# A recurrent layer on 8 cores: the hidden activations of the feed-forward stage transposed by DMA instead of by TensorE and ScalarE

## The chip, the cores and the metric

One Trainium2 chip, all 8 of its cores. Each core runs the same program on one of 8 sequences of 4096 tokens, with no traffic between cores. The metric is the device time of the slowest core in microseconds (us).

## What is computed

The layer is a spectral mixer times a gated feed-forward. The part that the change touches is the feed-forward with block quantisation:

```python
def block_quant(v, m_bits, bk):          # blocks of bk=32 along K share an exponent
    vb = v.reshape(*lead, K // bk, bk)
    amax = max(abs(vb)); e = floor(log2(amax)); scale = exp2(e - m_bits)
    return (round(vb / scale) * scale).reshape(v.shape)

def lowprec_linear(x, w, b, m_bits, bk):
    return einsum('bsk,nk->bsn', block_quant(x), block_quant(w)) + b

xn = layernorm(x)                        # (8, 4096, 1024)
h = gelu(lowprec_linear(xn, w_fc, b_fc)) # 1024 -> 4096
g = silu(lowprec_linear(h, w_proj, b_proj))   # 4096 -> 1024
out = x + spectral_mixer(xn) * g
```

The spectral mixer (a Fourier transform of chunks of 64 tokens, an attention over the low frequencies, a causal convolution over the high ones, and the inverse transform) is computed in later stages and is not changed.

## The kernel before

The program is written by hand: `B` collects for each engine a list of instructions in the order in which they are emitted, `b.wait` adds a wait on a semaphore to one engine's list, `b.inc` and `b.seal` add an increment. Every engine runs its list in order, so an instruction behind a wait waits too. SP is the engine whose queue issues nearly all DMAs; GpSimd issues a few later loads of weights. T, V and S are the semaphores that TensorE, VectorE and ScalarE raise.

The stages are: quantising and transposing the weights (lines 380 to 415), the feed-forward stage (lines 435 to 671), the Fourier stage and the convolution, the attention, and the inverse transform with the output. A full barrier stands between the first two and after the second.

The feed-forward stage runs over 32 tiles `i` of 128 tokens. All quantised weights are in SBUF (`WfcqT`, `WpjqT`). For each tile the 4096 hidden columns are taken in four quarters `w` of 1024:

- `hmm(w)`: up-projection of a quarter, 16 matmuls of 128x512 and two for the bias, from `xqT_t` into PSUM banks of `psA` (two quarters fit).
- `gelu(w)`: two ScalarE activations from PSUM into `hb_t` (two slots).
- `v_amax`, `q_scales`, `v_apply`: VectorE finds the block maxima, makes the scales, and writes the quantised bf16 quarter into `hq_t` (two slots), tokens on partitions.
- `t_tr(w)`: TensorE transposes the quarter by eight matmuls with the identity (`t_transpose8`, line 347) into PSUM banks 0 and 1 of `psB`.
- `s_te(w)`: ScalarE copies the eight blocks into `hqT_t` (`s_evac8`, line 357), hidden columns on partitions. `hqT_t` has one slot, 128x1024.
- `t_f(w)`: down-projection of the quarter, 16 matmuls of 128x512 that accumulate in banks 2 and 3 of `psB`, with `hqT_t` as weights; behind quarter 3 two for the bias.

TensorE's order in a tile is up-projections 0, 1, 2; transposes 0, down-projection 0, up-projection 3, transposes 1, down-projection 1, transposes 2, down-projection 2, transposes 3, down-projection 3, the transposes of the next tile's quantised input (`xq_t` to `xqT_t`), and then the next tile. ScalarE copies quarter 0 before GELU 2, and quarter 1 before GELU 3. VectorE quantises a quarter only after it has made the scales of the next. At the tile's end ScalarE applies SiLU to the sum, and SP stores it (`g_t` to `g_s`, line 670). SP also stores the normalised input (`xnb_t` to `xnb_s`, line 615) and loads the tile after next (`xt`, line 598). These three are all that SP issues in a tile.

Of the kernel before, what the change touches and what calls it, by code (L numbers as in the profile page):

```python
# [118 lines left out]
def build_program(phases=4, p2sub=9):  # L119
# [35 lines left out]
    def sb(name, shape, dtype, stack):  # L155
        return stack.enter_context(nc.sbuf_tensor(name, list(shape), dtype))
# [18 lines left out]

    b = B()
    for s in ("cst", "gq", "T", "V", "S", "wst0", "wst1", "x0", "x1",
              "xnbst", "gst", "p2x0", "p2x1", "p4l0", "p4l1", "p4s0", "p4s1", "bld", "bspl"):
        b.add_sem(s, esg.enter_context(nc.semaphore("sem_" + s)))

    def bankA(k, w=512):
# [2 lines left out]
    def bankB(k, w=512):  # L184
        return psB.ap()[:, 512 * k:512 * k + w]
# [111 lines left out]
    def q_views(src_ap, nblk, dst_ap, acol, tcol):  # L297
        W = 32 * nblk
        rs = rsq.ap()[:, acol:acol + nblk]
        sc = scq.ap()[:, acol:acol + nblk]  # L300
        return {
            "a": amx.ap()[:, acol:acol + nblk],
            "y": yq.ap()[:, acol:acol + nblk],
            "e32": e32q.ap()[:, acol:acol + nblk],
            "rs": rs, "sc": sc,
            "src3": src_ap.rearrange("p (nb k) -> p nb k", k=32),
            "tw": tb.ap()[:, tcol:tcol + W],
            "iw": ib.ap()[:, tcol:tcol + W],
            "t3": tb.ap()[:, tcol:tcol + W].rearrange("p (nb k) -> p nb k", k=32),
            "i3": ib.ap()[:, tcol:tcol + W].rearrange("p (nb k) -> p nb k", k=32),  # L310
            "dst3": dst_ap.rearrange("p (nb k) -> p nb k", k=32),
            "rs3": rs.unsqueeze(2).broadcast_to([128, nblk, 32]),
            "sc3": sc.unsqueeze(2).broadcast_to([128, nblk, 32]),
        }

    def q_amax(qv):
        b.plain("vector", lambda e: e.tensor_reduce(  # L317
            qv["a"], qv["src3"], axis=AX.X, op=AluOpType.max,
            apply_absolute_value=True))
        qv["vA"] = b.seal("vector", "V")  # L320

    def q_scales(qv):
        b.plain("vector", lambda e: e.drain())
        b.plain("vector", lambda e: e.tensor_scalar_max(qv["a"], qv["a"], 1e-37))
        b.plain("vector", lambda e: e.drain())
        b.plain("vector", lambda e: e.tensor_scalar(
            qv["e32"], qv["a"].bitcast(I32), 0x7F800000, None,
            op0=AluOpType.bitwise_and))
        b.plain("vector", lambda e: e.drain())
        b.plain("vector", lambda e: e.tensor_scalar_mul(  # L330
            qv["sc"], qv["e32"].bitcast(F32), 0.125))
        b.plain("vector", lambda e: e.drain())
        b.plain("vector", lambda e: e.reciprocal(qv["rs"], qv["sc"]))
        b.plain("vector", lambda e: e.drain())
        qv["sB"] = None

    def q_apply(qv):
        b.plain("vector", lambda e: e.tensor_tensor(  # L338
            qv["t3"], qv["src3"], qv["rs3"], op=AluOpType.mult))
        b.plain("vector", lambda e: e.drain())  # L340
        b.plain("vector", lambda e: e.tensor_copy(qv["iw"], qv["tw"]))  # L341
        b.plain("vector", lambda e: e.drain())
        b.plain("vector", lambda e: e.tensor_tensor(  # L343
            qv["dst3"], qv["i3"], qv["sc3"], op=AluOpType.mult))
        qv["done"] = b.seal("vector", "V")

    def t_transpose8(src_bf_ap):
        for blk in range(8):
            bank = blk // 4
            o = psB.ap()[:, 512 * bank + 128 * (blk % 4):  # L350
                         512 * bank + 128 * (blk % 4) + 128]
            sblk = src_bf_ap[:, 128 * blk:128 * blk + 128]
            b.plain("tensor", lambda e, o=o, l=sblk:
                    e.matmul(o, l, I128b.ap(), start=True, stop=True))  # L354
        return b.seal("tensor", "T")

    def s_evac8(dst_views, tT):
        b.wait("scalar", "T", tT)
        for blk in range(8):
            bank = blk // 4  # L360
            s = psB.ap()[:, 512 * bank + 128 * (blk % 4):
                         512 * bank + 128 * (blk % 4) + 128]
            b.plain("scalar", lambda e, o=dst_views[blk], s=s: e.copy(o, s))  # L363
        return b.seal("scalar", "S")
# [63 lines left out]
    hq_t = sb("hq_t", (128, 2048), BF16, es01)  # L428
    hqT_t = sb("hqT_t", (128, 1024), BF16, es01)
# [5 lines left out]
    chk = {}  # L435
# [71 lines left out]
    for i in range(NTILES):  # L507
# [41 lines left out]
                           hq_t.ap()[:, hs:hs + 1024], 32 + 32 * (w % 2), 0)  # L549

        def t_tr(w):
            b.wait("tensor", "V", chk[(i, w, "ap")])
            chk[(i, w, "tr")] = t_transpose8(hq_t.ap()[:, (w % 2) * 1024:
                                                       (w % 2) * 1024 + 1024])

        def s_te(w):
            chk[(i, w, "te")] = s_evac8(
                [hqT_t.ap()[:, 128 * j:128 * j + 128] for j in range(8)],
                chk[(i, w, "tr")])

        def t_f(w):
            b.wait("tensor", "S", chk[(i, w, "te")])
            if w == 0 and (i - 1, "sil") in chk:
                b.wait("tensor", "S", chk[(i - 1, "sil")])
            for K in range(8):
                lhs = hqT_t.ap()[:, 128 * K:128 * K + 128]
                for c2 in range(2):
                    rhs = WpjqT.ap()[:, D * (8 * w + K) + 512 * c2:
                                     D * (8 * w + K) + 512 * c2 + 512]
                    st = (w == 0 and K == 0)  # L570
                    b.plain("tensor", lambda e, o=bankB(2 + c2), l=lhs, r=rhs,
                            st=st: e.matmul(o, l, r, start=st, stop=False))  # L572
            if w == 3:
                for c2 in range(2):
                    rhs = bspl_pj.ap()[:, 512 * c2:512 * c2 + 512]
                    b.plain("tensor", lambda e, o=bankB(2 + c2), r=rhs:
                            e.matmul(o, ones2.ap(), r, start=False, stop=True))
            chk[(i, w, "f")] = b.seal("tensor", "T")
# [4 lines left out]
            chk[(i, w, "am")] = qh["vA"]  # L583

        def v_apply(w, qh):
            if (i, w - 2, "tr") in chk:
                b.wait("vector", "T", chk[(i, w - 2, "tr")])
            elif (i - 1, w + 2, "tr") in chk:
                b.wait("vector", "T", chk[(i - 1, w + 2, "tr")])
            q_apply(qh)  # L590
            chk[(i, w, "ap")] = qh["done"]

# [25 lines left out]
        v_amax(1, qh[1])  # L618
        q_scales(qh[1])
        v_apply(0, qh[0])  # L620
        t_tr(0)
        s_te(0)
        t_f(0)
        hmm(3)
        gelu(2)
        qh[2] = mk_qh(2)
        v_amax(2, qh[2])
        q_scales(qh[2])
        v_apply(1, qh[1])
        t_tr(1)  # L630
        s_te(1)
        t_f(1)
        gelu(3)
        qh[3] = mk_qh(3)
        v_amax(3, qh[3])
        q_scales(qh[3])
        v_apply(2, qh[2])
        t_tr(2)
        s_te(2)
        t_f(2)  # L640
        v_apply(3, qh[3])
        t_tr(3)
        s_te(3)
        t_f(3)
        if nx < NTILES:
            qx = q_views(xn_t.ap()[:, ((nx % 2) * 1024):((nx % 2) * 1024) + 1024],
                         32, xq_t.ap()[:, ((nx % 2) * 1024):((nx % 2) * 1024) + 1024],
                         0, 1024)
            q_amax(qx)
            q_scales(qx)  # L650
            if (i - 1, "xqT") in chk:
                b.wait("vector", "T", chk[(i - 1, "xqT")])
            q_apply(qx)
            b.wait("tensor", "V", qx["done"])
            b.wait("tensor", "S", chk[(i, 3, "te")])
            chk[(nx, "xqT")] = t_transpose8(
                xq_t.ap()[:, ((nx % 2) * 1024):((nx % 2) * 1024) + 1024])
            chk[(nx, "xqTe")] = s_evac8(
                [xqT_t.ap()[:, ((nx % 2) * 1024) + 128 * j:
                            ((nx % 2) * 1024) + 128 * j + 128] for j in range(8)],  # L660
                chk[(nx, "xqT")])
# [421 lines left out]
    for p in range(NPAIR):  # L1083
        sl = (p % 2) * 1024
# [111 lines left out]
```

How the kernel before makes its waits and increments, by code:

```python
    def inc(self, eng, make, sem, n=1):  # L88
        h = self.sem[sem]
        self.ops[eng].append(lambda e, make=make, h=h, n=n: make(e).then_inc(h, n))
        self.c[sem] += n
        return self.c[sem]
# [4 lines left out]
    def seal(self, eng, sem, n=1):  # L97
        h = self.sem[sem]
        last = self.ops[eng].pop()
        self.ops[eng].append(lambda e, last=last, h=h, n=n:
                             last(e).then_inc(h, n))
        self.c[sem] += n
        return self.c[sem]
# [1 line left out]
    def wait(self, eng, sem, val=None):  # L105
        h = self.sem[sem]
        v = self.c[sem] if val is None else val
        if v > 0:
            self.ops[eng].append(lambda e, h=h, v=v: e.wait_ge(h, v))
        return v
```

## Time and profile before

| | |
|---|---|
| time, median of 2 runs | 3848.76 us (3847.25 to 3850.28) |
| the profiled execution's own time | 3850.36 us |
| its span on the slowest core (core 5) | 3848.8 us |
| spans of the 8 cores | 3832.5 to 3848.8 us |
| busy: TensorE matmul, VectorE, ScalarE | 1897.9 (49%), 1584.8 (41%), 945.6 us (25%) |
| feed-forward stage | 672 to 2539 us |
| largest line of the chain that ended last | down-projection, L572: 12% |

The profile is that of one execution on the slowest core. Engines are PE (TensorE matmul), PEld (its weight loads), DVE (VectorE), ACT (ScalarE), POOL (GpSimd) and SP; SPq is SP's queue issuing a DMA. L572 is line 572 of the kernel; a helper's line stands for all that call it, so L354 is every transposing matmul and L363 every copy behind one. PEclk or the granted clock is TensorE's clock as a share of full speed (2.4 GHz).

### The profile page before, as it was taken

Reading aid. Unit: us, or ns where it says so; the run is one execution under the profiler, and the core shown is the slowest. Engines: PE = TensorE matmul, PEld = TensorE weight load, DVE = VectorE, ACT = ScalarE, POOL = GpSimd, SP = SyncE. Lnnn points to the kernel's source line nnn. Section 1 sums busy time; section 2 is a strip of 40 time slices with the busy share of each in tenths; the row PEclk is TensorE's granted clock in tenths of the full one; section 3 lists DMA queues with packets and bytes.
Section 4 is the critical chain, followed back from the end, with each engine's and each line's share of the span. In section 5 each row is a group of like instructions: output and inputs, shape, how many; then the busy total and the mean of one; then the engine's idle time right before and its main releaser. Section 6 shows DMA issues by size and latency. Waiting matters only on the chain.

```text
span 3848.8 us, 33385 instructions; the slowest of 8 cores (3832.5 to 3848.8 us)
## 1 busy us (share of the span) xinstructions
PE 1897.9 (49%) x10624; PEld 978.9 (25%) x10624; DVE 1584.8 (41%) x3175; ACT 945.6 (25%) x2925; POOL 29.9 (1%) x60
## 2 busy tenths in 40 slices
PE   0111101676676676676676667632777224233333
PEld 0000000222232232222222222222666212111211
DVE  4555554545445455455454554442233011221212
ACT  0111111333333323333333333310111032321111
POOL 0000000000000000000000000000000100000000
PEclk9999999888888888888888888865888655555555
DMA  1111111000000000000000000034010500014443
GB/s 43 55 55 55 50 54 55 25 25 17 28 22 20 28 21 21 28 18 24 28 14 28 28 14 28 14 72 104 23 29 23 88 0 1 0 43 143 143 144 139
DMA packets 62580, 168.28 MB, mean 44 GB/s; under 512 B 9923, under 2 KB 10179, under 8 KB 62408
## 3 DMA queue, kind: packets, MB, share of 16 engines
q1 hardware_dynamic: 54344, 151.47, 12.4%
q0 software_dynamic: 8064, 14.68, 2.5%
q8 instruction: 88, 1.44, 0.2%
q14 instruction: 84, 0.69, 0.1%
HBM read 138.84 MB, written 41.94 MB: 47 GB/s over the span
## 4 chain that ended last, share of the span: by engine, by line
PE 36%; DVE 23%; ACT 15%; DMA 14%; issue 7%; SPq 2%; DVEq 2%; POOL 1%; ACTq 0%; POOLq 0%
PE psB L572 12%; PE psA L525 7%; ACT hqT_t L363 5%; DMA gp<-g_s 4%; DVE tb L338 4%; DVE amx L317 4%; DMA wstg<-wproj 3%; PE psB L354 3%; DMA wstg<-wfc 3%; PE psA L857 3%; PE psB L875 3%; ACT hb_t L543 3%; DVE ib L341 2%; DVE hq_t L343 2%; DVE wqb L343 2%
## 5 line engine op out<-in xcount | busy, mean ns | idle before, releaser
L572 PE MATMUL psB<-WpjqT,hqT_t 128*128 128x512 bf16 x2048 | 592.4, 455 | 220.2 <-ACT hqT_t L363 220.2
L525 PE MATMUL psA<-WfcqT,xqT_t 128*128 128x512 bf16 x2048 | 505.7, 404 | 54.1 <-ACT xqT_t L363 54.1
L317 DVE TENSOR_REDUCE amx<-hb_t 128x32 f32<-128x1024 f32 x128 | 156.2, 1220 | 789.0 <-ACT hb_t L543 789.0
L363 ACT CAST hqT_t<-psB 128x128 bf16<-128x128 f32 x1024 | 186.2, 303 | 962.4 <-PE psB L354 962.3
L572 PEld LDWEIGHTS psB<-WpjqT,hqT_t 128*128 128x128 bf16 x2048 | 222.6, 113 | 554.6 <-issue 418.1
L354 PE MATMUL psB<-I128b_sb,wqb 128*128 128x128 bf16 x512 | 64.7, 306 | 597.7 <-DVE wqb L343 597.7
L525 PEld LDWEIGHTS psA<-WfcqT,xqT_t 128*128 128x128 bf16 x2048 | 203.2, 103 | 337.0 <-issue 143.1
L354 PE MATMUL psB<-I128b_sb,hq_t 128*128 128x128 bf16 x1024 | 102.1, 259 | 294.7 <-DVE hq_t L343 294.7
L354 PEld LDWEIGHTS psB<-I128b_sb,wqb 128*128 128x128 bf16 x512 | 49.5, 137 | 612.6 <-issue 612.6
L317 DVE TENSOR_REDUCE amx<-wstg 128x32 f32<-128x1024 f32 x64 | 78.1, 1220 | 251.5 <-DMA wstg<-wproj 129.0
L1135 DVE TENSOR_TENSOR ub<-psB,gp 128x1024 f32<-128x1024 f32 x32 | 39.2, 1225 | 329.7 <-PE psB L1129 329.7
L354 PEld LDWEIGHTS psB<-I128b_sb,hq_t 128*128 128x128 bf16 x1024 | 79.4, 116 | 345.6 <-issue 338.1
L1121 PE MATMUL psB<-xnb,I128b_sb 128*128 128x512 bf16 x64 | 32.4, 609 | 266.1 <-DMA gp<-g_s 266.1
L341 DVE CAST ib<-tb 128x1024 int32<-128x1024 f32 x224 | 155.5, 694 | 17.2 <-issue 0.9
L338 DVE TENSOR_TENSOR tb<-hb_t,rsq 128x1024 f32<-128x1024 f32 x128 | 156.7, 1224 | 14.2 <-issue 1.0
L343 DVE TENSOR_TENSOR hq_t<-ib,scq 128x1024 bf16<-128x1024 int32 x128 | 156.8, 1225 | 9.9 <-issue 0.4
L543 ACT ACTIVATE hb_t<-psA 128x512 f32<-128x512 f32 x256 | 145.1, 643 | 2.4 <-PE psA L529 1.7
L1112 ACT CAST slotR<-psA 66x512 bf16<-66x512 f32 x64 | 34.1, 582 | 357.5 <-PE psA L1102 357.5
L363 ACT CAST WfcqT<-psB 128x128 bf16<-128x128 f32 x256 | 46.5, 303 | 292.2 <-PE psB L354 292.2
L363 ACT CAST WpjqT<-psB 128x128 bf16<-128x128 f32 x256 | 46.6, 303 | 262.2 <-PE psB L354 262.1
L983 DVE TENSOR_TENSOR Ssb<-psB,maskt 128x256 f32<-128x256 f32 x64 | 24.2, 420 | 206.3 <-PE psB L976 206.3
L861 ACT ACTIVATE Hbt<-psA 128x232 bf16<-128x232 f32 x128 | 46.5, 364 | 253.2 <-PE psA L857 253.2
(122 smaller groups left out, 2461.9 us busy)
## 6 DMA issues: line engine op xcount, KB each, us to landing
wstg<-wfc SPq DMA_DIRECT2D x32, 512.0 KB, 3.5
wstg<-wproj SPq DMA_DIRECT2D x32, 512.0 KB, 3.7
xt<-x SPq DMA_DIRECT2D x32, 512.0 KB, 5.3
g_s<-g_t SPq DMA_DIRECT2D x32, 512.0 KB, 3.6
xnbp<-xnb_s SPq DMA_DIRECT2D x64, 256.0 KB, 2.6
xp<-x SPq DMA_DIRECT2D x32, 512.0 KB, 4.8
gp<-g_s SPq DMA_DIRECT2D x32, 512.0 KB, 5.3
out<-ob SPq DMA_DIRECT2D x32, 512.0 KB, 3.0
```

What stands on the lines that cost most here:

```text
L317: b.plain("vector", lambda e: e.tensor_reduce(qv["a"], qv["src3"], axis=AX.X, op=AluOpType.max, apply_absolute_value=True))
L338: b.plain("vector", lambda e: e.tensor_tensor(qv["t3"], qv["src3"], qv["rs3"], op=AluOpType.mult))
L341: b.plain("vector", lambda e: e.tensor_copy(qv["iw"], qv["tw"]))
L343: b.plain("vector", lambda e: e.tensor_tensor(qv["dst3"], qv["i3"], qv["sc3"], op=AluOpType.mult))
L354: e.matmul(o, l, I128b.ap(), start=True, stop=True))
L363: b.plain("scalar", lambda e, o=dst_views[blk], s=s: e.copy(o, s))
L525: st=(K == 0): e.matmul(o, l, r, start=st, stop=False))
L543: s=bankA(pb + c2): e.activation(o, s, AF.Gelu))
L572: st=st: e.matmul(o, l, r, start=st, stop=False))
L857: sp=(j == KS - 1): e.matmul(o, l, r, start=st, stop=sp))
L861: s=bankA(pb2)[:, 0:GW]: e.activation(o, s, AF.Gelu))
L875: sp=(K == 7): e.matmul(o, l, r, start=st, stop=sp))
```

## The change

The transposes of the quantised quarters leave TensorE and ScalarE. `t_tr` now issues eight DMA transposes of 128x128 bf16 from SP's queue, from `hq_t` to `hqT_t`, both in SBUF, on one of two new semaphores. Before the eight, SP waits until VectorE has written the quarter and until TensorE has ended the down-projection before it, since `hqT_t` still has one slot. `s_te` does nothing. `t_f` waits for the DMA semaphore in place of ScalarE's. `v_apply` may overwrite a slot of `hq_t` once the down-projection of two quarters ago has ended, where it waited for its transposes before. The transposes of the input tile (`xq_t`) stay on TensorE, without their wait for the copies of quarter 3.

```diff
     for s in ("cst", "gq", "T", "V", "S", "wst0", "wst1", "x0", "x1",
-              "xnbst", "gst", "p2x0", "p2x1", "p4l0", "p4l1", "p4s0", "p4s1", "bld", "bspl"):
+              "xnbst", "gst", "p2x0", "p2x1", "p4l0", "p4l1", "p4s0", "p4s1", "bld", "bspl",
+              "htr0", "htr1"):
...
         def t_tr(w):
-            b.wait("tensor", "V", chk[(i, w, "ap")])
-            chk[(i, w, "tr")] = t_transpose8(hq_t.ap()[:, (w % 2) * 1024:
-                                                       (w % 2) * 1024 + 1024])
+            sem = "htr%d" % (w % 2)
+            sl = (w % 2) * 1024
+            b.wait("sync", "V", chk[(i, w, "ap")])
+            if (i, w - 1, "f") in chk:
+                b.wait("sync", "T", chk[(i, w - 1, "f")])
+            elif (i - 1, 3, "f") in chk and w == 0:
+                b.wait("sync", "T", chk[(i - 1, 3, "f")])
+            for k in range(8):
+                b.inc("sync", lambda e, k=k, sl=sl: e.dma_start_transpose(
+                    hqT_t.ap()[:, 128 * k:128 * k + 128],
+                    hq_t.ap()[:, sl + 128 * k:sl + 128 * k + 128]), sem, 16)
+            chk[(i, w, "te")] = (sem, b.c[sem])
 
         def s_te(w):
-            chk[(i, w, "te")] = s_evac8(
-                [hqT_t.ap()[:, 128 * j:128 * j + 128] for j in range(8)],
-                chk[(i, w, "tr")])
+            pass
 
         def t_f(w):
-            b.wait("tensor", "S", chk[(i, w, "te")])
+            sem, v = chk[(i, w, "te")]
+            b.wait("tensor", sem, v)
...
         def v_apply(w, qh):
-            if (i, w - 2, "tr") in chk:
-                b.wait("vector", "T", chk[(i, w - 2, "tr")])
-            elif (i - 1, w + 2, "tr") in chk:
-                b.wait("vector", "T", chk[(i - 1, w + 2, "tr")])
+            if (i, w - 2, "f") in chk:
+                b.wait("vector", "T", chk[(i, w - 2, "f")])
+            elif (i - 1, w + 2, "f") in chk:
+                b.wait("vector", "T", chk[(i - 1, w + 2, "f")])
...
             b.wait("tensor", "V", qx["done"])
-            b.wait("tensor", "S", chk[(i, 3, "te")])
```

## Rows read from the trace of the kernel before

**Rows 1.** Stages: stretch, its length, PE, PEld, DVE, ACT, POOL busy, PEclk, DMA, GB/s

```profile
672.00:2539.00 1867.00, 1286.77 (x5696) 537.23 (x5696) 929.24 (x1438) 618.73 (x1852) 0.00 (x0) 0.83 0.07 22
...
3230.00:3849.00 619.00, 220.05 (x1104) 123.69 (x1104) 120.34 (x205) 121.94 (x276) 0.00 (x0) 0.54 0.27 95
```

**Rows 2.** The chain that ended last, over one tile: start us, us, what

```profile
1496.50 5.22 PE psA L525 x16
...
1515.18 1.24 DVE hq_t L343
...
1519.36 5.73 PE psB L572 x16
...
1528.55 0.53 PE psA L529 x2
...
1534.85 1.22 DVE tb L338
...
1536.92 1.24 DVE hq_t L343
...
1540.99 5.16 PE psB L572 x16
...
1548.29 3.61 PE psB L572 x16
1551.90 0.53 PE psB L577 x2
...
1554.68 5.14 PE psA L525 x16
```

**Rows 3.** Timeline of the same tile: start us, us, engine, line, what

```profile
1518.92 1.18 ACT L543 ACTIVATE hb_t<-psA 128x512 f32<-128x512 f32 x2
...
1519.75 0.15 PEld L572 LDWEIGHTS psB<-WpjqT,hqT_t 128*128 128x128 bf16 x1 [0.28 <-issue]
1520.17 0.15 PEld L572 LDWEIGHTS psB<-WpjqT,hqT_t 128*128 128x128 bf16 x1 [0.28 <-issue]
...
1530.99 1.18 ACT L543 ACTIVATE hb_t<-psA 128x512 f32<-128x512 f32 x2
```

**Rows 4.** The page's groups of instructions: busy, mean ns | idle before, releaser

```profile
L572 PE MATMUL psB<-WpjqT,hqT_t 128*128 128x512 bf16 x2048 | 592.4, 455 | 220.2 <-ACT hqT_t L363 220.2
...
L354 PE MATMUL psB<-I128b_sb,hq_t 128*128 128x128 bf16 x1024 | 102.1, 259 | 294.7 <-DVE hq_t L343 294.7
```

**Rows 5.** Two stretches of the tile, columns as in rows 1

```profile
1510.44:1519.36 8.92, 1.01 (x8) 0.80 (x9) 5.26 (x8) 1.70 (x9) 0.00 (x0) 0.67 0.08 29
1519.36:1529.08 9.72, 9.72 (x36) 3.72 (x36) 5.27 (x8) 0.74 (x2) 0.00 (x0) 0.78 0.01 2
```

**Rows 6.** Line 293, copies SBUF to SBUF of 2 KB: issue ns min/median/max, landing

```profile
L293 SPq DMA_DIRECT2D bspl_fc<-bst_hi x4: 497/497/617, 16.6 to 31.9; - x4
L293 SPq DMA_DIRECT2D bspl_fc<-bst_lo x4: 562/575/575, 17.2 to 32.4; - x4
...
DMA to landing us min/median/max: 1.6/1.7/1.7
```

**Rows 7.** Timeline of SP's queue, first in the prelude, then in a tile

```profile
21.63 0.50 SPq L293 DMA_DIRECT2D bspl_fc<-bst_hi  x1
22.17 0.57 SPq L293 DMA_DIRECT2D bspl_fc<-bst_lo  x1
22.79 0.51 SPq L220 DMA_DIRECT2D bst_f<-bfc  x1
...
1499.23 0.38 SPq L220 DMA_DIRECT2D xt<-x  x1
1510.10 0.32 SPq L615 DMA_DIRECT2D xnb_s<-xnb_t  x1
```

**Rows 8.** DMA issues by line: KB each, median us from issue to landing

```profile
xnb_s<-xnb_t SPq DMA_DIRECT2D x32, 256.0 KB, 2.0
```

**Rows 9.** DMA queues in the first 17 us: packets, MB, share of 16 engines

```profile
q1 hardware_dynamic: 3328, 0.41, 16.2%
```

## Prediction

> **What bounds the kernel now.** I began with the table of stages, the busy time of each engine in a stretch [rows 1]. The change touches only the feed-forward stage, 672 to 2539 us: 1867 us, in which TensorE is busy 1287, VectorE 929, ScalarE 619 and the DMA engines 7%. No engine fills it, so the stage is a chain that hands over from engine to engine. The chain of one token tile [rows 2] runs from the first matmul of the up-projection at 1496.50 to the same matmul of the next tile at 1554.68: 58.18 us, and 32 of them are 1862 us, the whole stage. So the question is what one tile's chain becomes, times 32.
>
> The reader should cut this chain into pieces. (a) 1496.50 to 1516.42, 19.92 us: up-projection 0, two GELUs with their table loads, scales, and the quantised hq_t of quarter 0 ready (1515.18 + 1.24). (b) hq_t ready to the start of down-projection 0 at 1519.36, 2.94 us: eight transposing matmuls and eight ScalarE copies. (c) down-projection 0, 5.73 us. (d) up-projection 3 behind it, 3.98 us, to 1529.07. (e) from there to hq_t of quarter 2 ready at 1538.16: the transposes and copies of quarter 1, then GELU 3 at 1530.99 [rows 3], then VectorE for 7.17 us. (f) 2.83 us of transposes and copies to down-projection 2 at 1540.99, 5.16 us long. (g) 2.14 us to down-projection 3 at 1548.29. (h) 4.15 us with its bias, to 1552.44. (i) 2.24 us for the transposes of the next input tile. The waits [rows 4] say the same in totals: TensorE stands 220.2 us for the copies into hqT_t and 294.7 us for hq_t.
>
> **The change, part by part.** A tile's 4096 hidden columns are done in four quarters. Removed: per quarter, eight 128x128 matmuls on TensorE and eight copies on ScalarE. In the chain they stand as 2.94 us (quarter 0), about 1.9 us ahead of GELU 3 (quarter 1: 1529.07 to 1530.99), 2.83 and 2.14 us. Their busy time is otherwise no gain, since neither engine is full [rows 1].
>
> Added: per quarter, eight DMA transposes from SP's queue, SBUF to SBUF, 32 KB each, 1024 in all. Call T the time from the moment they may start (hq_t ready and the earlier down-projection ended) to the moment the next down-projection may start, with all eight landed. It replaces (b), (f) and (g) directly.
>
> Moved: hqT_t is one buffer. Before, TensorE could put quarter w in PSUM and ScalarE copied it within 2 us. Now SP waits until down-projection w-1 has ended and only then starts eight transfers, so that from quarter 1 on T lies wholly between two down-projections. Only for quarter 1 is there cover: up-projection 3, 3.98 us of T. For quarters 2 and 3 hq_t is ready early if T is long, so T stands bare. TensorE works in order, so while it waits at down-projection 0, up-projection 3 waits too, and with it GELU 3.
>
> New chain of a tile. Down-projection 0 starts at 19.92 + T. Its end is 5.73 later. Down-projection 1 starts T after that end. Quarter 2's hq_t is ready 3.98 + 0.1 + 7.17 = 11.3 us after it (no copies ahead of GELU 3). With down-projection 1 at 5.7 us, the transposes of quarter 2 start at the later of 11.3 and T + 5.7: from T = 5.6 on, the down-projection sets it. Then T, 5.7, T, 5.7 + 0.55 of bias, and 2.24.
> For T over 5.6: 19.92 + 5.73 + 5.7 + 5.7 + 6.25 + 2.24 + 4T = 45.5 + 4T.
> For T under 5.6: 19.92 + 5.73 + 11.3 + 5.7 + 6.25 + 2.24 + 3T = 51.1 + 3T, which equals 58.2 at T = 2.3.
>
> The 5.7 is a choice. After the idle stretches before down-projections 0 and 2 the sixteen matmuls took 5.73 and 5.16 us, where they take 3.61 after 2.14 us of hand-over [rows 2]. The table of one tile shows why [rows 5]: in the stretch with the long idle time the granted clock fell to 0.67, and the projection after it started low (1.2 GHz) and rose to 2.4 on the way: one weight load to the next is 0.43 us there [rows 3]. With an idle stretch of T before each of them I give every down-projection the 5.7 us of the first. If the clock stays low throughout, sixteen take 16 x 0.43 = 6.9, about 1.1 us more for each of four. That is possible: the last stage, 36% busy in short bursts, was granted 0.54 [rows 1].
>
> **What is T?** No row shows a DMA transpose, so it needs two bounds. The nearest rows are copies SBUF to SBUF from the same queue, 2 KB each: 0.50 to 0.58 us of the queue for one, a pitch of about 0.6 us in a row, 1.6 to 1.7 us from issue to landing [rows 6, 7]. If eight transposes pipeline like that, T = 7 x 0.6 + 1.7 + 0.1 = 6.0. If one ends before the next begins, T = 8 x 1.7 = 13.6. Lower still would be the plain loads' and stores' 0.32 to 0.38 us of queue [rows 7]: 7 x 0.36 + 1.7 = 4.2. Higher would be a serial row of transfers that land as the 256 KB store does, 2.0 us [rows 8]: 16. Moving the bytes is not the limit by any row: in the first 17 us 3328 small packets took 16.2% of 16 engines, 13 ns each [rows 9].
> A transpose has to be cut up by the queue into more pieces than a copy of one row, so its issue should be longer than 0.6 us, but full serialisation would be the worst a queue does. I take the middle of 6.0 and 13.6, T = 9.8, which is 1.2 us for each transpose.
> That a transpose costs a queue more than its bytes is not shown by any row. The Trainium skill, VectorE: DVE Perf Modes, "The three transpose paths", gives 1309 ns for a 128x128 bf16 transpose by DMA against 390 ns on TensorE, and so speaks against this change. As an estimate from that page, 8 x 1.31 = 10.5 us for T, the total would be near 4790 us.
>
> Other queue effects. SP holds three plain transfers a tile: the store of xnb, the store of g and the next x load [rows 7]. The xnb store (1510.10) goes out before hq_t is ready, so it costs nothing; the g store and x load wait for SiLU, after the last transposes have landed, and x is needed a tile later. The waits that SP gains hold back only the g store and the x load, which have that slack. VectorE's new waits are for down-projections two back: quarter 3's quantisation starts when down-projection 1 ends and takes about 3.3 us (for quarter 2: 1534.85 to 1538.16), less than T + 5.7, so it is hidden. ScalarE loses copies and can run GELU 2 some 2.4 us earlier; only quarter 1's hq_t comes sooner, which does not count, since the single hqT_t holds its transposes back. The dropped wait for quarter 3's copies frees nothing: TensorE is in order behind down-projection 3.
>
> **Sum.** T = 9.8: 45.5 + 39.2 = 84.7 us a tile, 26.6 more than 58.2, times 32 = 850 us. The profiled execution took 3850.4 us by its own time (span 3848.8), 0.04% above the median of 3848.8. 3850 + 850 = 4700 us.
>
> **Rivals.**
> 1. The transposes pipeline as the small copies do, T = 6.0. For it: the 0.6 us pitch [rows 7]. Against: a transpose is more work for its queue. 45.5 + 24 = 69.5, +11.4 a tile, +364: 4215 us. At the plain transfers' pitch, T = 4.2: 51.1 + 12.6 = 63.7, +5.6: 4030 us.
> 2. They run one after another and the clock stays low: T = 13.6 and 1.1 more for each of four down-projections: 45.5 + 4.4 + 54.4 = 104.3, +46.2, +1477: 5330 us. For it: the clock of 0.54 in the last stage. Against: issue and landing overlap in every row of SP.
> 3. Worse than serial copies: T of 16 or more, each transpose taking 2 us: 45.5 + 4.4 + 64 = 113.9, +1785: 5640 us; and if each 2-byte element were a packet of its own, 1024 packets an engine at 13 ns are 14 us for one transpose, T over 100, many milliseconds. For it: nothing in the trace shows how the elements are cut.
> 4. The other side: the eight act as one transfer. If their issues cost the queue next to nothing and they land together as the 256 KB store does, T is 2.0 + 0.3 = 2.3, and 51.1 + 6.9 = 58.0 gives 3845 us, no change. Faster by 2% (77 us, 2.4 a tile) needs T below 1.5, under the landing time of a single 2 KB copy. Against it: no transfer left SP's queue for less than 0.32 us, and eight of those alone are 2.6 us.
> The Trainium skill, Advanced Engine Details and Errata, "X-Bar Transpose (TRN2)", says that transposing DMAs are as fast as regular ones, 350 to 400 GB/s; that is the rule behind this fourth rival, and no run shown here tests it.
>
> **Chances.** Forecast (T from 7 to 12) 0.50; rival 1 0.22; rival 2 0.12; rival 3 0.13; rival 4 0.03. Leaving out rival 3, rival 4 and the part of rival 1 below 6.0, the range is 4200 to 5330 us. About 2% (77 us) is what can be told from no change. Slower by over 2%: 0.97. Within: 0.02. Faster: 0.01.
>
> **What the changed profile would show.** The copies into hqT_t and the transposing matmuls on hq_t are gone. SP's queue shows 1024 transposes; their pitch is T's main term. A tile takes 85 us, the stage some 2710, and the rest of the kernel is as before. TensorE's idle time before the down-projection is ended by DMA of hqT_t, about 4 x 9.8 - 4 = 35 us a tile. The transposes of quarters 1 to 3 are issued right at the end of a down-projection. The down-projections take 5.2 to 6.9 us. I would be wrong if the pitch is well off 1.2 us; if SP issues quarter 2 or 3 on VectorE's word rather than TensorE's; or if other stages move.

## The result, and the profile after

The changed kernel takes 4827.3 us (median of 11 runs) against 3850.4 us for the kernel before (10 runs): ratio 1.255, 95% interval 1.252 to 1.259. It is 977 us slower, 30.5 us for each of the 32 tiles. The forecast was 4700 us in a range of 4200 to 5330.

All of it lies in the feed-forward stage. The table of stages of the profile after (columns as in [rows 1]: stretch, length, busy time of PE, PEld, DVE, ACT, POOL, PEclk, DMA share, GB/s):

```profile
672.00:3515.00 2843.00, 1262.90 (x4672) 473.16 (x4672) 926.62 (x1429) 436.79 (x825) 0.00 (x0) 0.75 0.10 26
3515.00:4825.00 1310.00, 547.91 (x4416) 392.62 (x4416) 307.52 (x1204) 230.81 (x558) 29.77 (x56) 0.61 0.24 70
```

The stage went from 1867 us [rows 1] to 2843, 976 us more, with ScalarE's busy time down from 619 to 437 us and TensorE's from 1287 to 1263. What follows the stage takes 1310 us in both. The engines got less work and the stage got longer: the mark of a chain.

The chain that ended last, over one tile of the profile after (start us, us, what; compare [rows 2]):

```profile
1495.10 1.24 DVE hq_t L344
1496.46 1.10 SPq L561
1497.61 1.22 SPq L561
...
1505.24 2.33 DMA hqT_t<-hq_t
...
1507.82 5.31 PE psB L581 x16
1513.20 1.09 SPq L561
...
1520.71 1.23 SPq L561
1521.99 2.33 DMA hqT_t<-hq_t
1524.45 5.53 PE psB L581 x16
...
1538.83 2.33 DMA hqT_t<-hq_t
1541.30 5.63 PE psB L581 x16
1547.00 1.09 SPq L561
...
1555.78 2.33 DMA hqT_t<-hq_t
1558.25 5.68 PE psB L581 x16
1563.93 0.53 PE psB L586 x2
...
1566.71 3.40 PE psA L526 x15
```

SPq L561 is SP's queue issuing one transpose. Read it as four repeats of one pattern: seven issues of 1.10 to 1.24 us at a pitch of 1.27 (1.14 behind the first), then the eighth transpose from its issue to its landing (2.33), then 0.1 to 0.3 us to TensorE, then a down-projection. From the end of down-projection 0 (1513.13) to the start of the next (1524.45) is 11.3 us, and 11.3 for the two behind it; for quarter 0, from hq_t ready, it is 11.5. Each group of issues begins 0.07 us after a down-projection has ended, and TensorE's up-projection 3 has vanished from the chain. Up-projection 0 of this tile began at 1478.02 and that of the next at 1566.71, so a tile is 88.7 us where it was 58.2 [rows 2].

The same in totals, for the tile hqT_t (minimum, median and maximum of the duration in ns, first and last start):

```profile
L561 SPq DMA_TRANSPOSE hqT_t<-hq_t x1024: 1093/1232/1317, 697.5 to 3504.9; - x171
...
  DMA hqT_t<-hq_t: 1522.5, 128
...
  DVE tb L339: 183.5, 32
DMA to landing us min/median/max: 2.2/2.3/3.3
```

TensorE stood 1522.5 us for transposes, where it stood 220.2 and 294.7 us for the copies and for hq_t [rows 4]. VectorE waited 183.5 us for down-projection 1 before it might overwrite hq_t, in time that the next transposes cover.

### The profile page after: what moved, and what is told of

Same layout as the page of the kernel before. It is cut to its first block, busy times and chain, and to the rows that moved or that the text cites. A ratio compares the mean times of both kernels' runs of the same rounds, so it can differ in the third digit from the quotient of the medians.

```text
span 4825.7 us, 31347 instructions; the slowest of 8 cores (4812.1 to 4825.7 us)
## 1 busy us (share of the span) xinstructions
PE 1875.5 (39%) x9600; PEld 915.3 (19%) x9600; DVE 1586.8 (33%) x3175; ACT 765.4 (16%) x1901; POOL 30.0 (1%) x60
## 4 chain that ended last, share of the span: by engine, by line
PE 28%; SPq 24%; DMA 17%; DVE 15%; ACT 8%; issue 6%; DVEq 1%; POOL 0%; ACTq 0%; POOLq 0%
SPq L561 23%; PE psB L581 15%; DMA hqT_t<-hq_t 6%; DMA gp<-g_s 3%; DMA wstg<-wproj 3%; DVE amx L318 2%; PE psA L526 2%; DVE tb L339 2%; PE psA L865 2%; DMA wstg<-wfc 2%; PE psB L883 2%; DVE wqb L344 2%; DMA xnbp<-xnb_s 1%; ACT hb_t L544 1%; DVE ib L342 1%
## 5 line engine op out<-in xcount | busy, mean ns | idle before, releaser
L581 PE MATMUL psB<-WpjqT,hqT_t 128*128 128x512 bf16 x2048 | 703.0, 519 | 1522.5 <-DMA hqT_t<-hq_t 1522.5
L581 PEld LDWEIGHTS psB<-WpjqT,hqT_t 128*128 128x128 bf16 x2048 | 247.5, 125 | 1978.1 <-issue 1904.7
L526 PE MATMUL psA<-WfcqT,xqT_t 128*128 128x512 bf16 x2048 | 466.0, 381 | 54.1 <-ACT xqT_t L364 54.1
L364 ACT CAST xqT_t<-psB 128x128 bf16<-128x128 f32 x256 | 46.5, 303 | 1458.6 <-PE psB L355 1458.6
L339 DVE TENSOR_TENSOR tb<-hb_t,rsq 128x1024 f32<-128x1024 f32 x128 | 156.9, 1225 | 197.8 <-PE psB L581 183.5
L334 DVE RECIPROCAL rsq<-scq 128x32 f32<-128x32 f32 x224 | 79.0, 353 | 18.2 <-issue 2.0
```

The lines of the kernel that those rows point to most:

```text
L339: b.plain("vector", lambda e: e.tensor_tensor(qv["t3"], qv["src3"], qv["rs3"], op=AluOpType.mult))
L526: st=(K == 0): e.matmul(o, l, r, start=st, stop=False))
```

## The experiments

My theory after this profile: SP's queue pays about 1.25 us for each transpose of 128x128, and the single slot of hqT_t keeps T from overlapping with any down-projection. Two questions: what is the 1.25 us the price of, and how much of the loss is price and how much is the slot?

**One transpose for eight.** The destination is already laid out as eight groups of 128 columns, so one instruction can do it:

```diff
-            for k in range(8):
-                b.inc("sync", lambda e, k=k, sl=sl: e.dma_start_transpose(
-                    hqT_t.ap()[:, 128 * k:128 * k + 128],
-                    hq_t.ap()[:, sl + 128 * k:sl + 128 * k + 128]), sem, 16)
+            b.inc("sync", lambda e, sl=sl: e.dma_start_transpose(
+                hqT_t.ap().rearrange("p (g r) -> p g r", g=8),
+                hq_t.ap()[:, sl:sl + 1024]), sem, 16)
```

> The changed kernel with one DMA transpose of 128x1024 per quarter in place of eight of 128x128; the same blocks land in the same places. In the changed kernel one transpose holds SP's queue for 1.23 us and T is 11.4 us. Theory (the price is per 128x128 block, paid in SP's queue): one instruction holds the queue for 8 x 1.23 = about 10 us, T stays 11 to 11.5 us, the time stays at 4827 us within 1%. Rival (the price is per instruction): the queue is held for 1.2 to 2 us, T falls to about 3 us, the tile to 58 or 59 us and the time to about 3850 us.

Measured: 3863.7 us, ratio 1.0038 (1.0025 to 1.0052). The theory as I had it was wrong and its rival right: the price is per instruction, at least from 32 to 256 KB. The issue durations and the landing of this run, for the tile hqT_t:

```profile
L560 SPq DMA_TRANSPOSE hqT_t<-hq_t x128: 1217/1218/1472, 698.9 to 2551.2; - x128
...
DMA to landing us min/median/max: 2.7/2.8/2.9
```

Eight times the data hold the queue for the same 1.22 us and land 0.5 us later. Its chain shows all of T: hq_t ends at 1528.45, and down-projection 0 starts 3.1 us later.

```profile
1527.21 1.24 DVE hq_t L344
...
1528.58 2.76 DMA hqT_t<-hq_t
...
1531.58 5.69 PE psB L580 x16
```

So 964 of the 977 us go away when the same bytes are issued as 128 instructions and not 1024, with slot, waits and order untouched.

**Two transposes of 128x512.**

```diff
-            for k in range(8):
+            for k in range(2):
                 b.inc("sync", lambda e, k=k, sl=sl: e.dma_start_transpose(
-                    hqT_t.ap()[:, 128 * k:128 * k + 128],
-                    hq_t.ap()[:, sl + 128 * k:sl + 128 * k + 128]), sem, 16)
+                    hqT_t.ap()[:, 512 * k:512 * k + 512].rearrange(
+                        "p (g r) -> p g r", g=4),
+                    hq_t.ap()[:, sl + 512 * k:sl + 512 * k + 512]), sem, 16)
```

> The changed kernel with two transposes of 128x512 per quarter. Theory (1.23 us of SP's queue for each instruction, whatever its size, and a landing of 2.3 to 2.8 us from its issue): T = 1.25 + 2.6 + 0.1 = 4.0 us, 1 us more than with one; in this range quarters 0, 2 and 3 count, 3 us a tile, 3864 + 96 = 3960 us. Rival (the cost rises more than in proportion, since several transposes in flight get in each other's way): over 4050 us.

Measured: 3950.5 us, ratio 1.026 (1.023 to 1.028). In its chain one issue of 1.20 us stands before a landing of 2.39:

```profile
1555.50 1.20 SPq L561
...
1556.75 2.39 DMA hqT_t<-hq_t
...
1559.38 5.83 PE psB L582 x16
```

T is 3.9 us. With one, two and eight instructions T is 3.0, 3.9 and 11.4 us: a pitch of 1.2 to 1.3 us for each instruction but the last, and one landing, which is 2.8 us for a transpose of 256 KB, 2.4 for 128 KB and 2.3 for 32 KB.

**Plain copies in place of transposes.** This kernel leaves the transposition out: eight plain DMA copies of the same blocks.

```diff
-                b.inc("sync", lambda e, k=k, sl=sl: e.dma_start_transpose(
-                    hqT_t.ap()[:, 128 * k:128 * k + 128],
-                    hq_t.ap()[:, sl + 128 * k:sl + 128 * k + 128]), sem, 16)
+                b.inc("sync", lambda e, k=k, sl=sl: e.dma_start(
+                    out=hqT_t.ap()[:, 128 * k:128 * k + 128],
+                    in_=hq_t.ap()[:, sl + 128 * k:sl + 128 * k + 128]), sem, 16)
```

> The changed kernel with eight plain DMA copies of 128x128 per quarter in place of the eight transposes, the same bytes from and to the same places; it leaves the transposition out, so its output is not the layer's. Theory (the price is that of the transposing instruction, 1.23 us of the queue, not of a small DMA in SBUF): plain copies hold the queue for 0.35 to 0.55 us, T = 7 x 0.5 + 1.8 = 5.3, the time 3864 + 32 x 3 x 2.3 = 4085 us, 4000 to 4150. Rival (any DMA of 128 rows of 256 bytes in SBUF costs the queue as much): T 11.4, 4827 us.

Measured: 4249.3 us, ratio 1.103 (1.100 to 1.105), above my 4000 to 4150. The chain of a quarter says why:

```profile
1547.97 0.47 SPq L561
1548.49 0.59 SPq L561
...
1552.36 1.83 DMA hqT_t<-hq_t
...
1554.44 1.87 PE psB L581 x4
```

The last row is the down-projection's start, cut off by the end of the window. A copy holds the queue for 0.60 us at a pitch of 0.65, close to what the small copies of the prelude had shown [rows 6, 7]; I had gone back to 0.5. T is 6.5 us, 1.2 more than I expected, which in three places a tile is 115 of the 164 us above my 4085. For the other 49 the page has a sign: the matmuls of the up-projections are busy 28 us more, and those of the down-projections 27, than with one transpose (506.7 against 478.7 us, 682.9 against 655.7). So the 977 us split: 399 us are paid when the eight transfers are plain copies, and 578 us more when each is a transpose, at twice the queue time and with 0.5 us more from issue to landing (2.3 against 1.8).

**The other queue.** The same eight transposes and waits, on ScalarE's queue.

```diff
-            b.wait("sync", "V", chk[(i, w, "ap")])
+            b.wait("scalar", "V", chk[(i, w, "ap")])
...
-                b.inc("sync", lambda e, k=k, sl=sl: e.dma_start_transpose(
+                b.inc("scalar", lambda e, k=k, sl=sl: e.dma_start_transpose(
```

> The changed kernel with the eight transposes of a quarter issued from ScalarE's queue in place of SP's, with the same waits. Theory (the 1.23 us belong to the instruction's issue, on whatever sequencer): 1.2 to 1.3 us for each, the tile as long as in the changed kernel or somewhat longer where GELU 2 now stands behind the eight issues of quarter 0 (quarter 1 is ready early enough), 4800 to 4900 us. Rival (it is SP's own slowness): the transposes hold ScalarE's queue for a third or a half of that, and the time falls well below 4500 us.

Measured, in one run: 4904.0 us beside 3861.8 for before. Its view of hqT_t:

```profile
L561 ACTq DMA_TRANSPOSE hqT_t<-hq_t x1024: 1108/1265/1368, 700.1 to 3572.3; - x171
```

1.27 us, so the price is not SP's own. The kernel is somewhat slower than from SP, and its chain shows why: the eighth issue of quarter 0 starts at 1527.89 and holds ScalarE's queue for 1.26 us, and GELU 2 follows at 1529.32, then VectorE, then the issues of quarter 1 and GELU 3 in the same way. Both queues at once were not tried: the Trainium skill, DMA: Bandwidth & Descriptors, "Silent corruption: two transposing streams in flight at once", says that two such streams can corrupt each other; no run here shows it.

**A second slot of hqT_t**, with the eight transposes kept:

```diff
-    hqT_t = sb("hqT_t", (128, 1024), BF16, es01)
+    hqT_t = sb("hqT_t", (128, 2048), BF16, es01)
...
-            if (i, w - 1, "f") in chk:
-                b.wait("sync", "T", chk[(i, w - 1, "f")])
-            elif (i - 1, 3, "f") in chk and w == 0:
-                b.wait("sync", "T", chk[(i - 1, 3, "f")])
+            if (i, w - 2, "f") in chk:
+                b.wait("sync", "T", chk[(i, w - 2, "f")])
+            elif (i - 1, w + 2, "f") in chk:
+                b.wait("sync", "T", chk[(i - 1, w + 2, "f")])
...
-                    hqT_t.ap()[:, 128 * k:128 * k + 128],
+                    hqT_t.ap()[:, sl + 128 * k:sl + 128 * k + 128],
...
-                lhs = hqT_t.ap()[:, 128 * K:128 * K + 128]
+                lhs = hqT_t.ap()[:, (w % 2) * 1024 + 128 * K:
+                                 (w % 2) * 1024 + 128 * K + 128]
```

> The changed kernel with a second slot for hqT_t, so that SP waits for the down-projection of two quarters ago. Theory (half of the loss is the single slot, which sets transposes and down-projections one after another): quarter 1 is transposed while down-projection 0 and up-projection 3 run, and the tile falls from 88.7 us to 18.3 + 11.4 + 5.2 + 4 + 7.3 (quarter 2 ready at 46.5), then two quarters of transposes of 10 us each, 1.4 to land, a down-projection of 6.2 and 2.3: 76.5 us, 4435 us in all. Rival (each down-projection waits for its own transposes whenever they start, so the slot does not matter): 4827 us.

Measured: 4464.3 us, ratio 1.160 (1.158 to 1.162). With a second slot 363 of the 977 us go away; the rest is queue time that the slot does not hide. The shares of slot and price overlap: with one instruction 964 us go away and the one slot stays. In its chain quarters 2 and 3 stand as sixteen issues in one row, at a pitch of 1.27 us, with down-projection 2 under them:

```profile
1590.25 1.23 SPq L561
1591.63 1.13 SPq L561
...
1599.17 1.23 SPq L561
1600.45 2.33 DMA hqT_t<-hq_t
```

**Up-projection 3 earlier**, in TensorE's idle time ahead of down-projection 0, in the changed kernel and in the kernel before:

```diff
         hmm(2)
         gelu(1)
+        hmm(3)
...
         t_f(0)
-        hmm(3)
```

> The changed kernel with up-projection 3 issued right behind up-projection 2, in TensorE's idle time ahead of down-projection 0. Theory (quarter 1's transposes, 11.4 us, cover the 4 us of up-projection 3 in full): no change, 4827 us within 1%. Rival (TensorE's order, up-projection 3 held behind a down-projection that waits for DMA, is part of the loss): 4 us a tile less, 4700 us.

Measured: 4825.6 us, ratio 1.253 (1.251 to 1.256) where the changed kernel has 1.255 (1.252 to 1.259). No change, as the theory had it: the transposes of quarter 1 had covered it. The timeline shows down-projection 1 still 11.1 us behind down-projection 0 with nothing in between:

```profile
1510.56 5.44 PE L581 MATMUL psB<-WpjqT,hqT_t 128*128 128x512 bf16 x16 [13.00 <-DMA hqT_t<-hq_t]
1527.13 5.68 PE L581 MATMUL psB<-WpjqT,hqT_t 128*128 128x512 bf16 x16 [11.13 <-DMA hqT_t<-hq_t]
```

> The kernel before with the same move of up-projection 3. Here the transposes of quarter 1 do not cover it. Theory: the copies of quarter 1 then start when VectorE has written it (1526.1 in the tile shown) and not behind up-projection 3, GELU 3 starts some 3 us earlier and quarter 2 is ready 3 us earlier: 32 x 3 = 96 us less, 3755 us. Rival (the chain is given back by a lower clock or by VectorE): no change, 3850 us.

Measured: 3724.9 us, ratio 0.968 (0.966 to 0.969), 125 us less where I had expected 96. The same line is worth nothing in one kernel and 3% in the other.

**One transpose, and the move.** One slot, one transpose per quarter, up-projection 3 early (both diffs above).

> One transpose of 128x1024 per quarter and up-projection 3 ahead of down-projection 0, but one slot of hqT_t. It parts what the order and the slot gave in the run with both (3503 us). Theory: with T = 3.0 us quarter 1's transpose no longer covers up-projection 3, so the move pays here where it paid nothing with eight; down-projections 0 to 3 each wait for T after the one before: 21.4 + 5.7 + 3 + 3.6 + 3 + 4.5 + 3 + 5 + 2.3 = 51.5 us a tile, 3850 - 32 x 6.7 = 3635 us, so that the order gives 230 us and the slot 130. Rival (the order alone gives all of it): 3503 us. Rival (the slot is needed for any gain): 3864 us.

Measured: 3680.2 us, ratio 0.951 (0.945 to 0.956), beside 3861.8 for before, which is 12 us more than it took beside the run with one transpose alone. The raw times make the order worth 184 us (3863.7 - 3680.2); the ratios (1.004 and 0.951) make it about 205, with 23 us of room either way. The time is 45 us above what I expected, or 25 us by the ratio, which is within that room. In the tile shown down-projection 1 ran long, 6.53 us where I had allowed 3.6, with a granted clock of 0.55; in the next tile it took 4.91 us, and that tile was 51.3 us long, where I expected 51.5.

```profile
1514.64 6.53 PE L580 MATMUL psB<-WpjqT,hqT_t 128*128 128x512 bf16 x16 [2.98 <-DMA hqT_t<-hq_t]
```

**One transpose, two slots, and the move.**

> The changed kernel with one transpose of 128x1024 per quarter, two slots of hqT_t, and up-projection 3 ahead of down-projection 0. With T = 3.0 us, as in the run with one transpose, nothing on TensorE or SP holds a quarter back: quarter 0 is ready 18.3 us into a tile, quarter 1 at 25.5, GELU 3 right then, quarter 2 at 32.5, quarter 3 at 36.2, down-projection 3 from 39 to 40 us on, at 6.2 with its bias and 2.3 to the next tile: 48 to 50 us a tile where before has 58.2. Theory (with the price per instruction paid once, the DMA path is shorter than TensorE's and ScalarE's): 3850 - 32 x 9 = 3560 us. Rival (the slot and the order do nothing more, because VectorE's chain and the low clock set the tile): 3725 us, as for the kernel before with the same move, or more.

Measured: 3503.4 us, ratio 0.909 (0.908 to 0.911). This kernel is 9% faster than before. The second slot gave 177 us of it by the raw times, about 160 by the ratios (0.951 and 0.909). Its chain from quarter 0 to 3 of a tile:

```profile
1505.86 1.24 DVE hq_t L344
...
1513.02 1.24 DVE hq_t L344
1514.33 1.09 ACT hb_t L544 x2
...
1520.17 1.24 DVE hq_t L344
...
1521.52 2.76 DMA hqT_t<-hq_t
...
1524.42 8.75 PE psB L581 x32
```

One transpose is left in the chain of a tile; before it the chain is VectorE's work with a GELU between two quarters. A quarter ends 7.15 us after the other.

**The same order without DMA.** The fair counterpart: the kernel before with up-projection 3 early and each GELU ahead of the copies.

```diff
         v_apply(1, qh[1])
         t_tr(1)
+        gelu(3)
         s_te(1)
         t_f(1)
-        gelu(3)
```

and the same for GELU 2 and quarter 0.

> The kernel before with up-projection 3 moved ahead of down-projection 0, and on ScalarE GELU 2 and GELU 3 ahead of the copies of quarters 0 and 1. VectorE gets each GELU's result 1.4 us earlier, the copies start 1.1 us later, and the down-projections behind them have slack. Theory: 2 x 1.4 us a tile less than with the move of up-projection 3 alone (3725 us): 3635 us. Rival (the later down-projections take back what the GELUs give): 3725 us.

Measured: 3548.5 us, ratio 0.921 (0.920 to 0.923), 86 us less than I expected. GELU 2 had stood 2.1 us behind hq_t with the move of up-projection 3 alone (not 1.4) and now stands 0.1 us behind it. The first two rows are of the run with the move alone, the others of this one:

```profile
1511.94 1.23 DVE L343 TENSOR_TENSOR hq_t<-ib,scq 128x1024 bf16<-128x1024 int32 x1
1515.28 1.18 ACT L543 ACTIVATE hb_t<-psA 128x512 f32<-128x512 f32 x2
...
1533.00 1.23 DVE L343 TENSOR_TENSOR hq_t<-ib,scq 128x1024 bf16<-128x1024 int32 x1
1534.32 1.09 ACT L543 ACTIVATE hb_t<-psA 128x512 f32<-128x512 f32 x2 [6.07 <-DVE hq_t L343]
```

GELU 3 gains as much (2.1 and 0.1 us), and two such gains are 32 x 4 = 128 us of the 176. That the remaining 48 came from down-projections that no longer follow a long idle stretch is what I read from the pages, not a thing I tested alone: one of their matmuls took 466 ns on average in the run with the move alone and 434 here, 66 us over 2048, of which not all lies in the chain. So 303 us of the 348 that the best kernel wins can be had with TensorE's transposes. The other 45 us come with the DMA transposes and the second slot together; this order with TensorE's transposes and two slots was not run, so they are not parted.

## Why the prediction was right

**The cut of the chain and the law 45.5 + 4T: right.** Four T a tile, from the second quarter on starting at the end of a down-projection; quarter 1's T covering up-projection 3; VectorE's new wait and the g store hidden. The run with up-projection 3 moved and the run with the second slot confirm the two places on which the law stands, cover and slot. With one and two instructions, T under 5.6, the other branch gives 51.1 + 3 x 3.0 = 60.1 a tile or 3911 us, and 51.1 + 3 x 3.9 = 62.8 or 3998 us, against 3864 and 3950 measured: 47 and 48 us high, 1.5 a tile, about what piece (a) is too long (below).

**T = 9.8: too small, 11.4 measured, and near it in part by luck.** I took the middle of two bounds, 6.0 and 13.6, with no row that shows a transpose, and called it 1.2 us a transpose. The pitch of 1.27 us is close to that; what 8 x 1.2 left out was the longer landing of the last one, 2.33 us from its issue, and some 0.2 to TensorE: 1.14 + 6 x 1.27 + 2.33 + 0.2 = 11.3, and 0.07 for SP to start. That is 1.6 us short, 6.4 a tile, 205 us in all.

**The pieces around it: about 2.3 us a tile too long.** Measured T (11.48 and three times 11.32, 45.4 in sum) in my law gives 90.9 us; the tile takes 88.7. Piece (a) shrank from 19.92 to 18.3 us, since up-projection 0 ran at full clock, and the down-projections took 5.3 to 5.7 us, a little under the 5.7 that I gave each. Two errors of opposite sign left 4700 against 4827.

**The reason that I gave for a long issue: wrong.** I wrote that the queue has to cut a transpose into more pieces than a copy, so that its issue grows. It does take twice as long as a copy's (1.23 against 0.60 us), but not for its pieces: the eight transposes of a quarter are 1280 packets, 160 each; the eight plain copies are 1152, 144 each, at half the queue time; and the one transpose is 1056 packets at the same queue time. What the 1.2 us is spent on, no run shows. Had I asked the price per instruction or per byte, the first question about this change would have been why there are eight.

**Rivals.** The first (pipelined at 0.6 us) is what plain copies do. The second (serial) is ruled out: the issues overlap with the landings, 1.27 us apart where a landing takes 2.3. The third had two forms, 2 us for each transpose and a packet for each element: the pitch is 1.27 us, and 160 packets are far from the 16384 elements of a block. The fourth, that the eight act as one, is what one instruction does: 3864 us, no change at my bound of 2%.

**The 1309 ns.** The measured 1232 ns of queue time are near the figure that the Trainium skill, VectorE: DVE Perf Modes, "The three transpose paths", gives for a 128x128 transpose by DMA; and with one block in each instruction the estimate 8 x 1.31 = 10.5 came nearer to 11.4 than my 9.8 did. But it can't be multiplied by the number of blocks: with all eight in one instruction T is 3.0.

## What to carry to other kernels

Price a DMA transpose by the instruction, not by the block. Here, up to 256 KB, it was 1.25 us of the queue for each, one landing of 2.3 to 2.8 us at the end, and data that hardly counts. Before a transfer takes the place of an engine's work, ask whether its destination is one buffer, for then nothing hides its latency. And take out cheap order faults first: moving one block of matmuls into idle time and two activations ahead of copies was worth 303 us of the 348 that the best kernel gained.

## What the runs showed of the hardware that I had not expected

A transposing DMA holds its queue about equally long for 32 KB and for 256 KB. The 1.23 and 1.22 us above are of different cores, and the core matters a little. In the changed kernel the median is 1232 ns on each even core and 1202 on each odd one. For one transpose of 256 KB it is 1233 ns on core 0 and 1218 on core 5, so the step in size adds 1 and 16 ns. On ScalarE's queue, core 4, 32 KB take 1265 ns. With eight, the DMA engines were nearly idle meanwhile. These are the queues' lines (packets, MB, share of 16 engines), first of the changed kernel in 12 us with eight transposes, then of the run with one transpose in 3.5 us around it:

```profile
q1 hardware_dynamic: 1280, 0.26, 10.2%
```

```profile
q1 hardware_dynamic: 1056, 0.26, 33.3%
GB/s 0 0 0 0 0 0 0 0 0 0 0 0 0 12 120 219 287 287 295 281 293 295 284 284 223 88 29 0 0 0 0 0 0 0 0 0 0 0 0 0
```

1280 packets against 1056 for the same bytes are 224 more, 32 for each of the seven additional instructions. As one instruction the data move at 280 to 295 GB/s in about 1 us, in packets under 512 bytes.

TensorE's clock did something that my steps did not foresee. In the kernel before, up-projection 0 took 5.14 to 5.22 us, behind a down-projection that had run at 3.61 [rows 2]. After, it took 3.61 us, behind one of 5.68: its line's busy time fell from 505.7 to 466.0 us in all. The granted clock was 1.00 over the first 13.94 us of the tile, where before has 0.88 over its first 13.94. That the slower down-projection ahead of it is the reason does not hold in the other runs. With plain copies down-projection 3 took 6.55 us and up-projection 0 behind it 5.30; with one transpose and the early up-projection 3 a down-projection of 3.61 us was followed by an up-projection 0 of 3.61:

```profile
1518.52 6.55 PE L581 MATMUL psB<-WpjqT,hqT_t 128*128 128x512 bf16 x16 [6.40 <-DMA hqT_t<-hq_t]
...
1527.84 5.30 PE L526 MATMUL psA<-WfcqT,xqT_t 128*128 128x512 bf16 x16 [1.69 <-ACT xqT_t L364]
```

```profile
1532.32 3.61 PE L580 MATMUL psB<-WpjqT,hqT_t 128*128 128x512 bf16 x16 [2.98 <-DMA hqT_t<-hq_t]
...
1538.72 3.61 PE L526 MATMUL psA<-WfcqT,xqT_t 128*128 128x512 bf16 x16 [1.70 <-ACT xqT_t L364]
```

What decides it stays open.
